# A causal attention stage that computes its own relative products, with the mask added on PE

## The chip, the cores and the metric

The kernel runs on one core of a Trainium2 chip. The metric is the time of one execution on the device in microseconds (us), as the median over several runs. The whole program is a decoder of four gated layers; the change touches only the attention of layer 0.

## The reference, cut to what matters

Layer 0's attention has 16 heads of 16 channels over 8 sequences of 512 rows. Queries come from the stream, keys and values from a context. To every score a relative term is added: the product of the query with a table `Er`, skewed so that the column says how far back the key lies. A causal mask follows, and the softmax.

```python
def _skew(QEr):
    B, H, R, C = QEr.shape
    padded = jnp.pad(QEr, ((0, 0), (0, 0), (0, 0), (1, 0)))
    reshaped = padded.reshape(B, H, C + 1, R)
    return reshaped[:, :, 1:, :]
# q, k, v: (8, 16 heads, 512, 16)
QEr = q @ Er.T
Srel = _skew(QEr)
attn = (q @ k.T + Srel) / 4      # then -inf where the key lies after the query
out = softmax(attn, axis=-1) @ v
```

## The kernel before, in words

The program is a row of phases, each with its own buffers and semaphores; a barrier of all engines ends each. Three phases bear on the change. There are 8 batches (sequences) of 16 heads, 128 heads in all, and a head has four query tiles t = 0..3 of 128 rows; by causality tile t has (t + 1) * 128 key columns, so its tiles are 128, 256, 384 and 512 wide.

**`qkv` (names `a_`).** For each batch it normalises the rows, makes Q and K transposed in four jobs (two of K, two of Q, 128 channels each), and splits each float32 result on DVE into three bf16 parts (L255 to L259, one after the other). `parts` has two buffers, so the split of job j waits until the store of job j - 2 has landed. SP stores a job with one DMA at L190. The dram tensors `k_parts` and `q_parts` hold the three parts one after the other.

**`rel_scores` (names `r_`).** A product of 96 rows stands for a float32 product of 16 channels: six pairs of bf16 parts (`TERMS`), 16 rows each, are stacked on the partitions. POOL loads Q for a batch with six DMAs, each onto 16 partitions (L1273). PE multiplies each of the four tiles of a head with the table (L1307), DVE and ACT copy two tiles each out of PSUM (L1333, L1354), and SP writes the head to the dram tensor `rel` (L1286), 128 x 1280 float32, 640 KB, through a ring of four buffers.

**`causal_attention` (names `t_`).** POOL loads Q and K, each with six DMAs onto 16 partitions (L3797), one pair every second head, and V (L3793). SP reads a head of `rel` back with the skew done by the address pattern (L3756), into one of four tiles `relsb`. POOL adds the mask `M` to the diagonal blocks of that tile (L3822). The rest is a software pipeline written out by hand in steps; step u stands for one tile of one head, u = 4 * head + t, and every engine walks through the steps in order:

- PE: the score product of unit u + 4 (L3850), the transposes of unit u (L3857), and at t = 1 four of the 16 value products of the group of four heads before (L3869).
- DVE: for unit u + 3 the sum of scores and relative part, with its row minimum (L3896); at t = 0 and 2 the copy of the transposed tile u out of PSUM (L3745); once per group the copy of the output (L3902).
- ACT: exp of unit u + 3 (L3923); at t = 1 and 3 the copy of the transposed tile (L3745).

The transposed tiles have two PSUM buffers, one for even and one for odd t. PE's transposes of unit u wait for the exp of u and for the copy of u - 2:

```python
wait(pe, "expo", u.n + 1)
wait(pe, "cp_act" if u.t % 2 else "cp_dve", u.head * 2 + u.t // 2)
```

Of the kernel before, what the change touches and what calls it, by code (L numbers as in the profile page):

```python
# [32 lines left out]
def alone(eng):  # L33

    eng.nop(nofuse=True)
# [97 lines left out]
def qkv(nc, G, name, src, jobs, weights, vjob, ctx=None, affine=None, tile_k=None, nlog=0):  # L133
# [11 lines left out]
    nj = len(jobs)  # L145
    scaled = sorted({(j[3], j[4]) for j in jobs if j[3] and j[4] != 1.0})
    with phase(nc, name, "w c0 c1 c_free stats rstd xn xn_free xt_ps xt_ps_free xt xt_free "
# [21 lines left out]
        with nc.Block() as block:  # L169

            @block.sync
            def _(sp):
# [33 lines left out]
                sp.wait_ge(s["parts_st0"], 16 + 16 * NB * ((nj + 1) // 2))  # L206
                sp.wait_ge(s["parts_st1"], 16 + 16 * NB * (nj // 2))
# [18 lines left out]
            def _(dve):  # L226
# [20 lines left out]
                def split(b, before):  # L247
                    ch.at(before)
                    for j in range(nj):
# [4 lines left out]
                        dve.wait_ge(s[f"parts_st{j % 2}"], b * (16 * k) + 16 * (j // 2) + 16)  # L254
# [122 lines left out]
def attention(nc, G, name, qs, ks, vs, H, DH, blocks, masks, odst, sums, rel=None):  # L377

    NC = max(1, 6 * DH // P + (6 * DH % P > 0)) if DH < 64 else 3
    TPC = 6 // NC
    KR = TPC * DH
    HD, VW = H * DH, DH + 1
    GH = 4
    NG = H // GH  # L400
    SCORES, EXPO, TURN = 7, 6, 4
    width = [(blocks(t)[1] - blocks(t)[0]) * P for t in range(NT)]
    OFF = [sum(width[:t]) for t in range(NT)]
    WMAX = max(width)

    users = [[t for t in range(NT) if blocks(t)[0] <= kb < blocks(t)[1]] for kb in range(NT)]
    windowed = WMAX < S
    UW = WMAX if windowed else S
    nload = 13
    with phase(nc, name, "in0 in1 loaded qk_free vh vones rel0 rel1 score least expo turned cp_dve cp_act pv "  # L410
               "o_free o_st0 o_st1") as (s, sb, ps):
        Q = sb("Q", [P, 2, NC, H, S], BF16)
        K = sb("K", [P, 2, NC, H, S], BF16)
        V = sb("V", [P, 2, NT, HD])
        Vh = sb("Vh", [P, GH, NT, VW])
        prob = sb("prob", [P, NT, WMAX])
        expT = sb("expT", [P, 2, NT * UW])
        nmax = sb("nmax", [P, 2, NT])
        osb = sb("osb", [VW, GH, S])
        if rel is not None:  # L420
            relsb = sb("relsb", [P, 2, sum(width)])
            summed = sb("summed", [P, NT, WMAX])
        sps = ps("sps", [P, NT, S])
        tps = ps("tps", [P, 2, S])
        ops = ps("ops", [VW, 2, S])

        class Unit:


            def __init__(self, p, it, h, j, t, n, pair, first):  # L430

                self.p, self.it, self.h, self.slot, self.t, self.n, self.pair, self.first = p, it, h, j % GH, t, n, pair, first

        def walk(eng, step, head):

            def early(m):
                def at(k):
                    h, t = divmod(m + k, NT)
                    return Unit(0, 0, h, h, t, h, h // 2, False) if m + k >= 0 else None
                return at  # L440

            def group(p, it, g, final):
                b = it * 2 + p
                for i in range(GH):
# [11 lines left out]
            for m in range(-SCORES, 0):  # L456
                step(early(m))
# [3746 lines left out]
```

## Time and profile before

| | |
|---|---|
| Median of 3 runs | 6249.43 us (6245.49 to 6275.58) |
| Profiled execution, first to last instruction | 6247.0 us |
| PE, DVE, ACT, POOL busy over the span | 74%, 63%, 46%, 33% |
| `qkv` of layer 0 | about 18 to 167 us |
| `rel_scores` | about 167 to 459 us |
| `causal_attention` | about 459 to 1079 us |
| all later phases | from 1079 us |

The profiled execution is 2.4 us shorter than the median of the runs. Busy shares over the whole span say little here, since the phases follow one another and the change reaches three of them; each has to be read in its own window.

### The profile page before, as it was taken

The page shows a single profiled execution, that of the slowest core. Times are in us where ns is not written, and L with a number is a line of the kernel's source. Part 1 is how long each engine was busy: PE and PEld are TensorE (multiplying, and loading weights), DVE is VectorE, ACT ScalarE, POOL GpSimd, SP SyncE. Part 2 cuts the span into 40 slices and gives each one's busy share as a digit, 9 for nine tenths or more (in the row PEclk, how much of TensorE's full clock was granted, in tenths as well). Part 3 has the DMA queues.
Part 4 walks back from the last instruction along what each step waited for, and adds up shares of the span by engine and source line. Part 5 has one row for each costly group of instructions (what it writes and reads, how often), then busy time and mean ns, then how long its engine had stood idle before and what let it go on. Part 6 is the DMA issues. An engine that isn't in the chain of part 4 may idle for free. (4 is left out here: it accounts for less than half of the span.)

```text
span 6247.0 us, 101680 instructions
## 1 busy us (share of the span) xinstructions
PE 4641.5 (74%) x24902; PEld 2868.6 (46%) x24902; DVE 3907.9 (63%) x8145; ACT 2867.3 (46%) x6151; POOL 2042.9 (33%) x3122
## 2 busy tenths in 40 slices
PE   7455666493879973998676767797677887995897
PEld 4113333342643331885234645686555663333433
DVE  6344555538547875443678956558866556886565
ACT  2235655215227753223564556435456323773353
POOL 0113443000036630221443554124542214542342
PEclk9558989696988986999778989998889998997897
DMA  4999986100063321111551232002321115332533
GB/s 158 283 360 190 211 197 157 45 0 0 0 201 89 97 63 45 43 43 41 155 144 62 102 115 65 27 13 92 129 73 41 28 49 182 92 85 82 179 117 100
DMA packets 317791, 648.30 MB, mean 104 GB/s; under 512 B 73170, under 2 KB 128115, under 8 KB 317384
## 3 DMA queue, kind: packets, MB, share of 16 engines
q1 hardware_dynamic: 245912, 450.68, 22.7%
q0 software_dynamic: 71488, 193.32, 13.1%
q8 instruction: 134, 2.20, 0.1%
q14 instruction: 257, 2.11, 0.1%
HBM read 373.99 MB, written 238.70 MB: 98 GB/s over the span
## 5 line engine op out<-in xcount | busy, mean ns | idle before, releaser
L1115 DVE TENSOR_REDUCE t_nmax<-t_aps 128x2 f32<-128x1024 f32 x700 | 838.0, 1221 | 278.2 <-PE t_aps L1037 272.6
L1222 ACT ACTIVATE t_expT<-t_bps 128x512 f32<-128x512 f32 x1290 | 700.9, 599 | 284.4 <-PE t_bps L1056 235.4
L1056 PE MATMUL t_bps<-t_Q,t_K 51*128 51x512 f32 (+2 forms) x1290 | 525.9, 468 | 60.8 <-ACT t_expT L1222 43.8
L1037 PE MATMUL t_aps<-t_K,t_Q 49*128 49x512 f32 (+2 forms) x1400 | 464.7, 460 | 64.7 <-DMA t_K<-k_halves 28.9
L1056 PEld LDWEIGHTS t_bps<-t_Q,t_K 51*128 51x128 f32 (+2 forms) x1290 | 228.8, 189 | 528.6 <-ACT t_expT L1222 373.5
L2517 DVE TENSOR_TENSOR f_hl<-f_h,f_hh 128x512 fp32r<-128x512 f32 x192 | 203.7, 1061 | 413.3 <-ACT f_hh L2442 413.3
L1083 PE MATMUL t_ops<-t_expT,t_V 128*17 128x512 f32 (+1 forms) x2560 | 414.2, 614 | 0.5 <-ACT t_expT L1222 0.4
L3923 ACT ACTIVATE t_relsb<-t_relsb,t_nmax 128x128 f32<-128x128 f32 (+3 forms) x515 | 277.6, 559 | 272.8 <-DVE t_nmax L3896 264.0
L3857 PE MATMUL t_tps<-ident,t_relsb 128*128 128x128 f32 x1280 | 246.6, 296 | 160.1 <-ACT t_expT L3745 149.3
L2806 POOL TENSOR_TENSOR a_crossed<-a_qsb,a_tab 128x256 f32<-128x256 f32 x272 | 268.1, 1007 | 295.9 <-ACT a_qsb L2753 271.3
L1156 POOL DMA_DIRECT2D t_Q<-q_halves x525 | 270.9, 518 | 143.9 <-POOLq L78 72.9
L3822 POOL TENSOR_TENSOR t_relsb<-t_relsb,t_M 128x128 f32<-128x128 f32 (+1 forms) x384 | 198.5, 546 | 335.5 <-DMA t_relsb<-rel 304.0
L3896 DVE CUSTOM_DVE_ANT_0 t_relsb<-t_sps,t_relsb 128x128 f32<-128x128 f32 (+3 forms) x515 | 234.0, 484 | 83.6 <-PE t_sps L3850 52.6
L3573 ACT ACTIVATE t_prob<-t_summed,t_nmax 128x256 f32<-128x256 f32 (+1 forms) x560 | 265.6, 479 | 26.9 <-DVE t_nmax L3625 22.3
L3857 PEld LDWEIGHTS t_tps<-ident,t_relsb 128*128 128x128 f32 x1280 | 169.0, 150 | 231.4 <-issue 215.7
L1156 POOL DMA_DIRECT2D t_K<-k_halves x525 | 267.5, 512 | 18.6 <-issue 10.3
L3515 PE MATMUL t_tps<-ident,t_prob 128*128 128x128 f32 x964 | 151.7, 303 | 154.4 <-DVE t_prob L3640 154.3
L3583 ACT COPY t_expT<-t_tps 128x512 f32<-128x512 f32 (+1 forms) x276 | 144.3, 523 | 262.6 <-PE t_tps L3515 262.6
L1037 PEld LDWEIGHTS t_aps<-t_K,t_Q 49*128 49x128 f32 (+2 forms) x1400 | 214.5, 199 | 103.8 <-issue 52.4
L1307 PE MATMUL r_o<-r_erk,r_Q 96*128 96x128 bf16 (+3 forms) x512 | 161.0, 460 | 133.2 <-DVEq L1335 92.8
L3745 DVE COPY t_expT<-t_tps 128x128 f32<-128x128 f32 (+1 forms) x256 | 108.0, 422 | 197.9 <-PE t_tps L3857 197.7
L2382 PE MATMUL f_yps<-f_wdh,f_hh 128*128 128x256 f32 x768 | 217.9, 284 | 13.8 <-DVE f_hl L2517 13.8
(441 smaller groups left out, 12543.1 us busy)
## 6 DMA issues: line engine op xcount, KB each, us to landing
rel<-r_out SPq DMA_DIRECT2D x128, 640.0 KB, 5.4
t_relsb<-rel SPq DMA_DIRECT2D x128, 640.0 KB, 5.6
t_Q<-q_halves POOLq DMA_DIRECT2D x420, 64.0 KB, 2.5
t_K<-k_halves POOLq DMA_DIRECT2D x420, 64.0 KB, 2.5
k_halves<-a_parts SPq DMA_DIRECT2D x48, 512.0 KB
q_halves<-a_parts SPq DMA_DIRECT2D x48, 512.0 KB, 5.6
o_xT<-attended SPq DMA_DIRECT2D x32, 512.0 KB, 4.3
f_R<-combine SPq DMA_DIRECT2D x128, 128.0 KB, 3.0
```

What stands on the lines that cost most here:

```text
L1037: last = nc.tensor.matmul(aps[:, (t * PPG + i) % 2, x, :], operand(Qr, KA, p, h, slice(t * P, (t + 1) * P)), operand(Kr, KA, p, h, slice(0 ...
L1056: nc.tensor.matmul(bps[:, slot_of(kb, j), :], operand(Kr, KB, p, h, slice(kb * P, (kb + 1) * P)), operand(Qr, KB, p, h, slice(0, S)), star ...
L1083: last = nc.tensor.matmul(ops[j * COL:j * COL + VW, :], V[:, p, kb, g * HG + j, :], expT[:, kb % RING, j, :], start=kb == 0, stop=kb == NT ...
L1115: nc.vector.tensor_reduce(nmax[:, g, t, i * HPT:(i + 1) * HPT], aps[:, (t * PPG + i) % 2], AX.X, ALU.max, negate=True).then_inc(s["maxed"], 1)
L1156: pool.dma_start(dst[o + i * DH:o + (i + 1) * DH, p, cols], rows(src, part, r, g, b)).then_inc(sem, 16)
L1222: nc.scalar.activation(expT[:, kb % RING, j, :], bps[:, slot_of(kb, j), :], ACT.Exp).then_inc(s["expo"], 1 + (PAD if end else 0))
L2382: last = nc.tensor.matmul(o, fast(x), fast(w), start=m == 0 and i == 0 and t % 2 == 0, stop=m == NF - 1 and i == 2, skip_group_check=True)
L2806: last = nc.gpsimd.tensor_tensor(y[:, :, k, :], x[:, :, 1 - k, :], tab[:, 2 * i + 1, t, k * HW:(k + 1) * HW].unsqueeze(1).broadcast_to([P, ...
L3573: nc.scalar.activation(prob[:, u.slot, i, x, 0:w], summed[:, u.slot, i, x, 0:w], ACT.Exp, scale=-1.0, bias=nmax[:, u.slot, i, x:x + 1], ac ...
L3857: last = nc.tensor.transpose(tps[:, u.t % 2, kb * P:(kb + 1) * P], u.tile()[:, kb * P:(kb + 1) * P], G.ident[:, :])
L3896: nc.vector.tensor_tensor_reduce(out=u.tile(), in0=sps[:, u.t, 0:u.w], in1=u.tile(), scale=1.0, scalar=3.0e38, op0=ALU.add, op1=ALU.min, a ...
L3923: nc.scalar.activation(u.tile(), u.tile(), ACT.Exp, scale=-1.0, bias=nmax[:, u.j, u.t:u.t + 1]).then_inc(s["expo"], 1)
```

## The change: what it does

`rel_scores` and `causal_attention` become one phase, `relative_attention`. On the same steps u, PE now also computes a relative product, that of unit u + 24 (six heads ahead, `AHEAD = 6`), after the transposes; its four tiles are taken in the order 3, 1, 0, 2 and go to two PSUM buffers. `keep_rows` copies them out at the end of a step: on DVE the tiles of 512 and 128 columns, on ACT those of 256 and 384. SP writes a head (`spill`, three buffers `rows`), and two heads later reads it back skewed (`skew`, five tiles `relsb`). The scores have three PSUM buffers in place of four, the output one in place of two.

POOL no longer adds the mask. For each score tile PE computes the diagonal block apart and accumulates onto it the product of an identity with the mask.

`qkv` stores a job with six DMAs, which write the six stacked terms of every head to `k_terms` or `q_terms`, [16 heads, 96, 4096]. Q and K are then loaded with four DMAs each of 96 partitions and four heads, and Q once and not twice. The loops are written out; the empty instruction behind each wait (`alone`) is gone. The old general `attention` function, which nothing called, is deleted.

```diff
 # qkv, SP: the store of one job
-                        sp.dma_start(dst.rearrange("r f t -> f r t")[row:row + P, :, ds(b * S, S)],
-                                     parts[:, j % 2]).then_inc(s[f"parts_st{j % 2}"], 16)
+                        h = row // 16
+                        for i, term in enumerate(TERMS):
+                            part = term[dst is not qdst] - 1
+                            sp.dma_start(dst[h:h + P // 16, i * 16:(i + 1) * 16, ds(b * S, S)], parts[:, j % 2, part]).then_inc(s[f"parts_st{j % 2}"], 16)
...
-def rel_scores(nc, G, name, qs, er, rel):
...
-def causal_attention(nc, G, name, qs, ks, vs, rel, odst, sums):
+def relative_attention(nc, G, name, qs, ks, vs, er, rel, odst, sums):
...
+    AHEAD = 6
+    SB, RS, RING = 3, 3, 5
+    ORDER = (3, 1, 0, 2)
...
+        def keep_rows(eng, op, n, i, what):
+
+            t = ORDER[i]
+            wait(eng, f"st{n % RS}", 16 * (n // RS))
+            eng.wait_ge(s["product"], n * NT + i + 1)
+            op(rows[:, n % RS, OFF[t]:OFF[t] + WIDTH[t]], rps[:, i % 2, 0:WIDTH[t]]).then_inc(s[what], 1)
...
+                def spill(n):
+                    if n >= NH:
+                        return
+                    sp.wait_ge(s["kept_d"], n * 2 + 2)
+                    sp.wait_ge(s["kept_a"], n * 2 + 2)
+                    sp.dma_start(rel[n:n + 1, :].rearrange("o (p c) -> (o p) c", c=RW), rows[:, n % RS, :]).then_inc(s[f"st{n % RS}"], 16)
+
+                def skew(n):
+                    if not 0 <= n < NH:
+                        return
+                    sp.wait_ge(s[f"st{n % RS}"], 16 * (n // RS + 1))
+                    wait(sp, "turned", (n - RING + 1) * NT)
+                    x = rel[n:n + 1, P - 1:]
+                    sp.dma_start(relsb[:, n % RING, :], bass.AP(x.tensor, x.offset, [[RW - 1, P], [1, RW]])).then_inc(s[f"rel{n % RING}"], 16)
...
+                for n in range(NH + 2):
+                    spill(n)
+                    skew(n - 2)
...
-                    qp, kp = TERMS[r]
-                    for dst, part, src in ((Q, qp, qs), (K, kp, ks)):
-                        pool.dma_start(dst[r * DH:(r + 1) * DH, p], src[part - 1].rearrange("(h d) t -> d h t", d=DH)[:, :, ds(b * S, S)]).then_inc(s[f"in{p}"], 16)
+                    if r < 2 * QH:
+                        dst, src, what = ((Q, qs, "q"), (K, ks, "k"))[r // QH]
+                        h = r % QH * (H // QH)
+                        pool.dma_start(dst[:, p, h:h + H // QH, :], src.rearrange("h r t -> r h t")[:, h:h + H // QH, b * S:(b + 1) * S]).then_inc(s[f"{what}{p}"], 16)
...
-                    wait(pe, "least", u.n - NT + 1)
-                    nc.tensor.matmul(sps[:, u.t, 0:u.w], Q[0:KR, u.p, u.h, u.t * P:(u.t + 1) * P], K[0:KR, u.p, u.h, 0:u.w],
-                                     start=True, stop=True).then_inc(s["score"], 1)
+                    wait(pe, "least", u - SB + 1)
+                    q, diag = Q[:, b % 2, h, t * P:(t + 1) * P], sps[:, u % SB, t * P:(t + 1) * P]
+                    if t:
+                        nc.tensor.matmul(sps[:, u % SB, 0:t * P], q, K[:, b % 2, h, 0:t * P], start=True, stop=True)
+                    nc.tensor.matmul(diag, q, K[:, b % 2, h, t * P:(t + 1) * P], start=True, stop=False)
+                    nc.tensor.matmul(diag, G.identb[:, :], G.masks[:, 2, :], start=False, stop=True).then_inc(s["score"], 1)
...
+                def relative(u):
+                    n, i = unit(u)
+                    if n is None:
+                        return
+                    b, h = divmod(n, H)
+                    t = ORDER[i]
+                    if h == 0 and i == 0:
+                        pe.wait_ge(s[f"q{b % 2}"], 16 * QH * (b // 2 + 1))
+                    wait(pe, "kept_a" if i % 2 else "kept_d", n * 2 + i // 2)
+                    nc.tensor.matmul(rps[:, i % 2, 0:WIDTH[t]], Q[:, b % 2, h, t * P:(t + 1) * P], erk[:, S - WIDTH[t]:S],
+                                     start=True, stop=True).then_inc(s["product"], 1)
...
+                def step(u):
+                    scores(u + SCORES)
+                    turn(u)
+                    relative(u + AHEAD * NT)
+                    n, t = unit(u)
+                    if n is not None and t == 1 and n >= HG:
+                        values(n // HG - 1, n % HG)
...
             @block.scalar
+                def step(u):
+                    n, t = unit(u + EXPO)
+                    if n is not None:
+                        act.wait_ge(s["least"], u + EXPO + 1)
+                        nc.scalar.activation(tile(n, t), tile(n, t), ACT.Exp, scale=-1.0, bias=nmax[:, n % RING, t:t + 1]).then_inc(s["expo"], 1)
+                    n, t = unit(u)
+                    if n is not None and t % 2:
+                        copied(act, nc.scalar.copy, n, t, "cp_act")
+                    m, i = unit(u + AHEAD * NT - 1)
+                    if m is not None and i % 2:
+                        keep_rows(act, nc.scalar.copy, m, i, "kept_a")
```

On PE, in the middle of the attention, one head before reads so (`t_sps` are the scores, `t_tps` the transposed tiles, `t_ops` the output; the register instructions of the loop stand between):

```order
L3850 MATMUL t_sps<-t_K,t_Q 128x256
L3857 MATMUL t_tps<-ident,t_relsb 128x128 x2
L3869 MATMUL t_ops<-t_expT,t_Vg 17x384 x4
L3733 REGISTER_ALU
L3850 MATMUL t_sps<-t_K,t_Q 128x384
L3733 REGISTER_ALU
L3857 MATMUL t_tps<-ident,t_relsb 128x128 x3
```

The same steps t = 1 and t = 2 on PE after the change (`t_rps` are the relative products):

```order
L3407 MATMUL t_sps<-t_K,t_Q 128x128
L3408 MATMUL t_sps<-t_K,t_Q 128x128
L3409 MATMUL t_sps<-masks,identb 128x128
L3418 MATMUL t_tps<-ident,t_relsb 128x128 x2
L3430 MATMUL t_rps<-t_erk,t_Q 128x256
L3442 MATMUL t_ops<-t_expT,t_Vg 17x128 x4
L3407 MATMUL t_sps<-t_K,t_Q 128x256
L3408 MATMUL t_sps<-t_K,t_Q 128x128
L3409 MATMUL t_sps<-masks,identb 128x128
L3418 MATMUL t_tps<-ident,t_relsb 128x128 x3
L3430 MATMUL t_rps<-t_erk,t_Q 128x128
```

Between the two transposes of step 1 and the three of step 2 there is now a relative product, and the one score product has become three.

On ACT one head in the same place before the change, exps and copies of transposed tiles:

```order
L3923 ACTIVATE t_relsb<-t_relsb,t_nmax 128x384
L3745 COPY t_expT<-t_tps 128x4x128
L3923 ACTIVATE t_relsb<-t_relsb,t_nmax 128x512
L3923 ACTIVATE t_relsb<-t_relsb,t_nmax 128x128
L3745 COPY t_expT<-t_tps 128x2x128
L3923 ACTIVATE t_relsb<-t_relsb,t_nmax 128x256
```

And after it, with the relative rows copied to `t_rows`:

```order
L3510 ACTIVATE t_relsb<-t_relsb,t_nmax 128x384
L3312 COPY t_expT<-t_tps 128x4x128
L3510 ACTIVATE t_relsb<-t_relsb,t_nmax 128x512
L3319 COPY t_rows<-t_rps 128x384
L3510 ACTIVATE t_relsb<-t_relsb,t_nmax 128x128
L3312 COPY t_expT<-t_tps 128x2x128
L3510 ACTIVATE t_relsb<-t_relsb,t_nmax 128x256
L3319 COPY t_rows<-t_rps 128x256
```

Two copies have come in, one between the exps of 512 and 128 columns, one after that of 256.

## Rows read from the trace of the kernel before

**Rows 1.** The page's head; busy time (instructions) of each engine by window, clock, DMA, GB/s.

```profile
span 6247.0 us, 101680 instructions
...
core 0: us, PE busy (x) PEld busy (x) DVE busy (x) ACT busy (x) POOL busy (x), PEclk, DMA share, GB/s
18.00:167.00 149.00, 125.58 (x384) 66.34 (x384) 109.96 (x256) 40.04 (x65) 10.15 (x16) 0.93 0.44 146
167.00:459.00 292.00, 160.98 (x512) 53.67 (x512) 116.32 (x261) 96.44 (x256) 30.54 (x55) 0.50 0.97 331
459.00:501.00 42.00, 0.50 (x3) 0.39 (x4) 1.21 (x3) 0.00 (x0) 10.02 (x18) 0.50 0.97 150
501.00:1079.00 578.00, 399.00 (x2818) 219.81 (x2816) 332.89 (x1318) 349.67 (x771) 257.13 (x504) 0.93 0.83 194
```

**Rows 2.** The same view: short stretches with one kind of transfer under way.

```profile
87.00:88.00 1.00, 1.00 (x5) 0.66 (x4) 0.97 (x2) 0.02 (x1) 0.00 (x0) 1.00 0.71 254
...
182.00:190.00 8.00, 0.00 (x0) 0.00 (x0) 0.00 (x0) 0.00 (x0) 0.84 (x2) 0.50 1.07 112
...
210.00:222.00 12.00, 10.02 (x32) 3.33 (x32) 6.92 (x16) 5.98 (x16) 0.00 (x0) 0.50 1.02 422
...
1020.00:1050.00 30.00, 20.41 (x154) 11.35 (x154) 18.04 (x75) 18.95 (x43) 12.16 (x25) 1.00 0.51 164
```

**Rows 3.** Timeline, one head period: start, duration, engine, line, out<-in, [idle before <-releaser].

```profile
1063.45 0.41 PE L3857 MATMUL t_tps<-ident,t_relsb 128*128 128x128 f32 x2 [1.16 <-ACT t_expT L3745]
1063.79 0.84 PE L3869 MATMUL t_ops<-t_expT,t_Vg 128*17 128x384 f32 x8
...
1064.56 0.34 PE L3850 MATMUL t_sps<-t_K,t_Q 96*128 96x384 bf16 x1
...
1064.73 0.49 PE L3857 MATMUL t_tps<-ident,t_relsb 128*128 128x128 f32 x3
...
1065.33 0.56 DVE L3745 COPY t_expT<-t_tps 128x384 f32<-128x384 f32 x1 [1.84 <-PE t_tps L3857]
...
1065.80 0.55 DVE L3896 CUSTOM_DVE_ANT_0 t_relsb<-t_sps,t_relsb 128x384 f32<-128x384 f32 x1
...
1066.45 0.61 ACT L3923 ACTIVATE t_relsb<-t_relsb,t_nmax 128x384 f32<-128x384 f32 x1 [1.57 <-DVE t_nmax L3896]
...
1066.98 0.56 ACT L3745 COPY t_expT<-t_tps 128x512 f32<-128x512 f32 x1
...
1067.44 1.01 ACT L3923 ACTIVATE t_relsb<-t_relsb,t_nmax 128x512 f32<-128x512 f32 x2
...
1067.68 0.41 PE L3857 MATMUL t_tps<-ident,t_relsb 128*128 128x128 f32 x2 [1.16 <-ACT t_expT L3745]
```

**Rows 4.** Groups by shape in `rel_scores` and in the attention (count | busy, mean ns | idle).

```profile
L1333 DVE COPY r_out<-r_o 128x512 f32<-128x512 f32 x122 | 83.0, 680 | 0.0
...
L1354 ACT COPY r_out<-r_o 128x384 f32<-128x384 f32 x122 | 59.2, 485 | 0.0
...
L3850 PE MATMUL t_sps<-t_K,t_Q 96*128 96x128 bf16 x126 | 29.3, 232 | 55.1 <-POOLq L3812 49.2 <-issue 5.9
```

**Rows 5.** Who waited for whom, 480 to 1060 us: total, times, longest.

```profile
DVE t_expT L3745 <- PE t_tps L3857: 190.9, 114, 3.3
PE t_tps L3857 <- ACT t_expT L3745: 145.8, 135, 2.1
...
DVE t_relsb L3896 <- POOL t_relsb L3822: 28.7, 20, 3.5
```

**Rows 6.** DMA issues and us to landing, 168 to 466 us.

```profile
rel<-r_out SPq DMA_DIRECT2D x128, 640.0 KB, 5.4
...
r_Q<-q_parts POOLq DMA_DIRECT2D x48, 256.0 KB, 10.7
```

**Rows 7.** The writes of `rel` alone, time to landing.

```profile
DMA to landing us min/median/max: 5.0/5.4/14.2
```

**Rows 8.** `qkv`: two jobs on DVE in the timeline, then the stores' landings.

```profile
83.29 0.42 DVE L255 CAST a_parts<-a_q 128x512 bf16<-128x512 f32 x1
...
86.40 0.43 DVE L255 CAST a_parts<-a_q 128x512 bf16<-128x512 f32 x1 [0.33 <-DVE a_parts L259]
...
89.58 0.43 DVE L255 CAST a_parts<-a_q 128x512 bf16<-128x512 f32 x1 [0.37 <-DMA k_parts<-a_parts]
...
DMA to landing us min/median/max: 3.2/3.2/3.9
```

**Rows 9.** SP issues DMAs back to back; the end of the attention (timeline).

```profile
18.58 0.46 SPq L177 DMA_DIRECT2D a_wk<-in_L_xattn_Wk  x1
19.08 0.46 SPq L177 DMA_DIRECT2D a_wv<-in_L_xattn_Wv  x1
...
1078.43 0.69 DVE L3902 COPY t_osb<-t_ops 128x512 f32<-128x512 f32 x1 [3.62 <-PE t_ops L3869]
```

**Rows 10.** The start of `rel_scores` (timeline).

```profile
171.73 0.41 DVE L1321 CAST r_pbf<-r_r 16x512 bf16<-16x512 f32 x1
172.45 2.89 POOL L1267 DMA_DIRECT2D r_erk<-r_pbf  x6 [4.64 <-DVE r_pbf L1321]
175.49 4.11 POOL L1273 DMA_DIRECT2D r_Q<-q_parts  x7 [0.15 <-issue]
...
193.02 2.33 PE L1307 MATMUL r_o<-r_erk,r_Q 96*128 96x128 bf16 x8 [35.91 <-DMA r_Q<-q_parts]
```

More of the change, by code:

```diff
@@ L129, in _, with qkv @@
                 sp.wait_ge(s["stored"], 16)
[L133 removed]
+def qkv(nc, G, name, src, jobs, weights, vjob, qdst, ctx=None, affine=None, tile_k=None, nlog=0):
     nj = len(jobs)
+    ST = 16 * len(TERMS)
     scaled = sorted({(j[3], j[4]) for j in jobs if j[3] and j[4] != 1.0})
@@ L3715, in walk @@
[L3715 to L3728 removed]
+        rps = ps("rps", [P, 2, S])
@@ new lines, in walk, with unit, copied @@
+        def walk(step):
+            for u in range(-(AHEAD + 1) * NT, NH * NT):
+                step(u)
+        def unit(u):
+            return divmod(u, NT) if 0 <= u < NH * NT else (None, None)
+        def copied(eng, op, n, t, what):
+            g = n // HG
+            if n % HG == 0 and t < 2:
+                wait(eng, "pv", g - 1)
+            eng.wait_ge(s["turned"], n * NT + t + 1)
+            x = expT[:, g % 2, n % HG, t * P:t * P + 1]
+            dst = bass.AP(x.tensor, x.offset, [list(x.ap[0]), [PITCH, t + 1], [1, P]])
+            op(dst, tps[:, t % 2, 0:WIDTH[t]].rearrange("p (k q) -> p k q", q=P)).then_inc(s[what], 1)
@@ L3883, in _, with link @@
+                pe.wait_ge(s["erp"], 96)
+                walk(step)
                 for kb in range(NT):
-                    values(NB * NG - 1, 1, kb)
+                    values(NGT - 1, kb)
             @block.vector
             def _(dve):
-                nc.vector.tensor_copy(M[:, :], G.masks[:, 2, :]).then_inc(s["mask"], 1)
-                nc.vector.memset(ops[:, :, :], 0.0).then_inc(s["zero"], 1)
+                def link(ins, n):
+                    ins.then_inc(s["chain"], 1)
+                    dve.wait_ge(s["chain"], n)
@@ L3915, in _ @@
-                keep(NB * NG - 1, 1, NB // 2 - 1, NB * NG // 2 - 1)
+                    n, t = unit(u)
+                    if n is None:
+                        return
+                    if t == 0:
+                        dve.wait_ge(s[f"rel{n % RING}"], 16 * (n // RING + 1))
+                    dve.wait_ge(s["score"], u + 1)
+                    nc.vector.tensor_tensor_reduce(out=tile(n, t), in0=sps[:, u % SB, 0:WIDTH[t]], in1=tile(n, t), scale=1.0, scalar=3.0e38,
+                                                   op0=ALU.add, op1=ALU.min, accum_out=nmax[:, n % RING, t:t + 1]).then_inc(s["least"], 1)
@@ L3917, in _ @@
+                walk(step)
+                keep(NGT - 1)
             @block.scalar
             def _(act):
-                def step(at):
-                    u = at(EXPO)
-                    if u:
-                        wait(act, "least", u.n + 1)
-                        nc.scalar.activation(u.tile(), u.tile(), ACT.Exp, scale=-1.0, bias=nmax[:, u.j, u.t:u.t + 1]).then_inc(s["expo"], 1)
-                    u = at(0)
-                    if u and u.t % 2:
-                        copied(act, nc.scalar.copy, u, "cp_act")
@@ L3931, in normalise_turn @@
+                walk(step)
 def normalise_turn(nc, G, name, src, dst):
```

617 lines of the change are left out of this document (105 added, 512 removed).

## The prediction

> **What bounds the kernel now.** I read the windows by phase first [rows 1]. Between 167 and 459 us the DMA engines are busy 0.97 of the time and PE only 161 of 292 us: `rel_scores` is bound by its transfers. From 459 to 501 us no engine computes, and again the DMA share is 0.97: the loads of the first batch. From 501 to 1079 us no engine is full: PE 399, ACT 350, DVE 333 of 578 us, DMA 0.83. Such a phase is bound by a loop of waits between engines, so I read the waits next: DVE waits 191 us for transposed tiles, PE waits 146 us for ACT's copies of them, and only 29 us go to the late relative tile [rows 5].
>
> The timeline shows the loop [rows 3]. PE's two transposes (t = 1) start at 1063.45, the value products at 1063.79, the score at 1064.56, the three transposes at 1064.73, DVE's copy of them at 1065.33, the next sum at 1065.80, its exp at 1066.45, ACT's copy of the 512 tile at 1066.98, and that frees the buffer for the transposes of the next head at 1067.68. The period is 0.34 + 0.77 + 0.17 + 0.60 + 0.47 + 0.65 + 0.53 + 0.70 = 4.23 us. The real mean from 501 to 1079 us is 578 / 128 = 4.5 us a head [rows 1]: some heads wait for a tile from POOL (28.7 / 128 = 0.22 us each [rows 5]), and the clock is at 0.93, not 1.00.
>
> Of the transfers I read three rates [rows 2]. Writes of `rel` run at 422 GB/s. Skewed reads alone give 164 GB/s at a share of 0.51, so 320 GB/s while they run. Loads of Q onto 16 partitions run at only 112 GB/s and keep the engines at 1.07: 3.1 MB of Q and K for a batch take 28 us of all the DMA engines. The Trainium skill ("SBUF — State Buffer", The DMA port swizzle) says that partitions 0 to 15 reach 4 of 16 ports and measured 104 GB/s; this trace agrees with its 112 GB/s. By that page 96 partitions reach all ports and the new loads should run nearly three times as fast.
>
> **What goes.** The three windows from 167 to 1079 us, 912 us [rows 1].
>
> **What it costs now: the new loop.** Relative product i of a head waits for the copy of product i - 2. The one that matters is i = 1 (256 columns), which stands on PE between the transposes of step 1 and the value products. It waits for ACT's copy of the 384-wide product (i = 3), and ACT does this one after the exp of the 512 tile, after the copy of the 512 tile. So the old link "ACT copy starts to transposes start, 0.70, and 0.34 more to the values" becomes: copy to exp 0.46 [rows 3], exp of 512 columns 0.62 (the pair takes 1.01 [rows 3]; I give the 128 one 0.39), copy of 384 columns 0.485 [rows 4] and 0.13 for the signal (0.70 less the copy's 0.56, rounded): 1.70 us in place of 1.04, +0.66.
>
> The relative product itself occupies PE for about 0.12 us (a 384-wide score frees PE after 0.17 [rows 3]). The score of this step has the same 384 columns plus a mask product. No row shows a mask product: below it costs 128 columns, 0.06 us, above an isolated product of that width, 0.232 us [rows 4]; it stands back to back with others, so I take 0.12 with the split. Every fourth head DVE's copy of the output (0.69 [rows 9]) stands before the sum of the 512 tile and delays its exp by about 0.4: 0.1 a head. The loop is 4.23 + 0.66 + 0.12 + 0.12 + 0.10 = 5.2 us. The other relative products fall in PE's idle time ahead of the freed buffer, 1.16 us a head [rows 3].
>
> Engine work stays under this: DVE has 332.9 / 128 = 2.6 us a head plus 0.68 and 0.29 for its rows, 3.6; ACT 2.7 plus 0.86, 3.6; PE 3.1 plus four products and four masks, at most 8 x 0.232, 5.0 if nothing overlaps, about 4 if it does. The mask leaves POOL (257 us of work) and gains nothing by itself, as POOL waited for its loads most of the time; only the 0.22 us of late tiles may shrink. I let these and the slower stretches of the clock stand at +0.1: **5.3 us a head**.
>
> DMA per head: write 655 KB at 422 GB/s 1.55 us; skewed read at 320 GB/s 2.05; Q and K 197 KB, between 112 GB/s (1.75) and the 358 GB/s of 1 KB stores (254 at a share of 0.71 [rows 2]; 0.55), and I take 0.8; V and output 0.1. That is 4.5 us, below 5.3, with ends of 4.25 and 5.45.
>
> **Start and end.** Today the first product comes 26 us after the phase begins, held by the loads of Q [rows 10]. Now Q is issued at once and the table's chain ends near 178 us. Head 0 is written after 3 us, lands 5.4 us later [rows 6], and is read back in some 6: the first sum about 24 us into the phase. Then 122 heads at 5.3 and the last six, which have no relative products left, at 4.3: 672 us. The last value products and copy take about 5 [rows 9]. New phase: 24 + 672 + 5 = 701 us against 912: **-211**.
>
> **`qkv`.** DVE takes 3.1 us for a job (83.29 to 86.40) and a store lands in 3.2, so with two buffers it waits 0.37 us [rows 8]. Now six DMAs carry 786 KB. The fixed part of the landing is 3.2 less 393 KB at 358 GB/s, 2.1 us. Below, the transfer is as long as six issues on SP, five spacings of 0.50 us [rows 9] and the last piece at 358 GB/s, 2.9: job 2 of a batch waits about 1.5 us more, +12 us over 8 batches. Above, it runs at the 112 GB/s of the slow loads, 7.0 us a job: 28 for the jobs and 2.9 for the other megabyte make 31 us a batch against today's 17.5 to 18, +105. Neither shape is like the new one (8 x 16 x 512), and I take the middle, 4.7 us: job 2 starts 6.8 after job 0's end, job 3 4.7 after that, and a batch takes 22.5 us, +5, so **+40**.
>
> The Trainium skill ("DMA: Bandwidth & Descriptors", Why a DMA increments its semaphore by 16 and not by 1) has a rule against this change: a DMA runs on the largest number of engines up to 16 that divides the slowest dimension of both sides. Here these are 8 and 128, so 8 engines would serve each store. At half of 358 GB/s that is 4.4 us a job and about +37 us; by the plain rate of the rows the term would be +12 and the whole 28 us better. No row before shows such a shape.
>
> Sum: 6247 - 211 + 40 = 6076 us for the profiled execution, about 6078 as a median of runs (2 us more, as today).
>
> **The rivals.**
> - *The wait for ACT's copy doesn't bind* (the removed empty instructions shorten each handover, or signals overlap). Then the loop is the old one plus 0.24: 4.5 us a head, 122 x 0.8 = 98 us less: 5980. For it: three handovers in the loop, each with 0.1 or more. Against: the order of instructions is strict. 0.15.
> - *The transfers bind.* If 1 KB pieces and not the 16 partitions are what is slow, Q and K cost 1.75 us a head and all DMA 5.45; with bursts (writes wait up to 14.2 us today [rows 7]) 5.9 us a head: +73, 6150. For it: the DMA share of 0.83 to 0.97 in all windows from 167 us. Against: 1 KB stores ran at 358 GB/s [rows 2]. 0.20.
> - *Slower than before: the round trip through `rows`.* A head's four copies are spread over three steps, 0.75 of a head period, and the slot is needed again after 3 periods, so a write must land within 2.25 periods. The gain is gone when the period reaches 5.3 + 169 / 122 = 6.7, that is when writes land in 15 us on average, and at 15.7 us it is slower by over 0.5%. The median is 5.4, the maximum 14.2 [rows 7], under the slow loads. SP also queues each skewed read behind the next write's wait, so a late copy delays both. 0.06; about 6300.
> - *Little is moved* (the two phases' costs add up again, 6.5 us a head): 6220 to 6280. 0.04.
>
> **Numbers.** The likeliest case (0.55) is 6078, with its own range of 6040 (stores at the lower bound) to 6140 (stores between middle and upper). With half of the first rival and nearly all of the second the range is 5975 to 6170. Below 0.5% (31 us) a measurement of this kernel tells little from no change. Faster by more than that: 0.55 + 0.15 + 0.20, and a little of the rest, 0.91; within it 0.03; slower 0.06.
>
> **What would show it.** In the new profile: ACT's copy of the 384 product is what PE's relative product of 256 columns waits for, about 0.5 us or more a head; DVE's longest wait stays the one for transposed tiles; heads come every 5.3 us; the loads of Q and K land in well under 10.7 us [rows 6] and DMA is near 0.85, not 1.0. In `qkv` DVE waits for the stores by some 5 us a batch. The prediction is wrong if the period is set by the skewed read or by the write of `rows` (DVE or ACT waiting on a DMA), if PE's work and not a wait fills the loop, or if `qkv` grows by 12 or by 100 us.

## The result, and the profile after

| | before | after |
|---|---|---|
| Median of runs | 6255.79 us (4 runs) | 6079.80 us (6057.82 to 6096.23, 4 runs) |
| Profiled execution | 6247.0 us | 6056.2 us |
| Ratio, with its 95% interval | | 0.9717 (0.9688 to 0.9747) |

The change makes the kernel 2.8% faster; 6078 was predicted. The profiled execution after is the fastest of its four.

The windows of the changed kernel come first, in the columns of [rows 1]: `qkv`, the start of `relative_attention` up to its first sum, and from the first to the last sum. The last row is a stretch of `qkv` in which only the new stores run.

```profile
18.00:220.00 202.00, 137.58 (x384) 71.94 (x384) 109.93 (x256) 40.14 (x65) 10.15 (x16) 0.81 0.54 170
220.00:249.00 29.00, 9.07 (x30) 2.77 (x30) 8.34 (x19) 4.25 (x10) 10.80 (x17) 0.50 0.91 256
249.00:892.00 643.00, 494.02 (x4146) 291.31 (x4145) 422.65 (x1551) 424.34 (x1010) 54.55 (x94) 0.96 0.88 303
...
90.00:99.00 9.00, 8.93 (x30) 4.73 (x28) 5.57 (x15) 1.37 (x2) 0.41 (x2) 1.00 0.51 155
```

`qkv` now ends at 220 us and not at 167: 53 us lost. The attention ends with DVE's last copy of the output at 898.8 us (1079.1 before [rows 9]), so all that lies between the end of `qkv` and there takes 679 us and not 912: 233 won. Together that is 180 us. The profiled execution is 191 us shorter; the other 11 us lie in later phases whose code is the same, and are scatter between two executions (the runs of either kernel lie up to 38 us apart).

One head period of the changed kernel, from the timeline of all engines, to be held against [rows 3]:

```profile
640.88 0.56 ACT L3312 COPY t_expT<-t_tps 128x512 f32<-128x512 f32 x1
...
641.34 0.72 ACT L3510 ACTIVATE t_relsb<-t_relsb,t_nmax 128x512 f32<-128x512 f32 x1
...
641.59 0.41 PE L3418 MATMUL t_tps<-ident,t_relsb 128*128 128x128 f32 x2 [0.45 <-ACT t_expT L3312]
641.97 0.47 ACT L3319 COPY t_rows<-t_rps 128x384 f32<-128x384 f32 x1
...
642.49 0.28 PE L3430 MATMUL t_rps<-t_erk,t_Q 96*128 96x256 bf16 x1 [0.49 <-ACT t_rows L3319]
...
642.70 0.84 PE L3442 MATMUL t_ops<-t_expT,t_Vg 128*17 128x384 f32 x8
...
643.47 0.28 PE L3407 MATMUL t_sps<-t_K,t_Q 96*128 96x256 bf16 x1
...
643.71 0.50 PE L3418 MATMUL t_tps<-ident,t_relsb 128*128 128x128 f32 x3
...
644.25 0.56 DVE L3312 COPY t_expT<-t_tps 128x384 f32<-128x384 f32 x1 [1.76 <-PE t_tps L3418]
...
644.72 0.55 DVE L3482 CUSTOM_DVE_ANT_0 t_relsb<-t_sps,t_relsb 128x384 f32<-128x384 f32 x1
...
645.31 0.62 ACT L3510 ACTIVATE t_relsb<-t_relsb,t_nmax 128x384 f32<-128x384 f32 x1 [1.65 <-DVE t_nmax L3482]
...
645.83 0.57 ACT L3312 COPY t_expT<-t_tps 128x512 f32<-128x512 f32 x1
```

From one copy of the 512 tile (640.88) to the next (645.83) are 4.95 us. The reader is to see the row at 642.49: the transposes ahead of it were done, but PE stands 0.49 us until ACT has copied the 384 columns of the relative product, and the value products, the next scores and the next transposes are queued behind.

The waits from 260 to 880 us (in total, times, longest) say the same for all heads:

```profile
DVE t_expT L3312 <- PE t_tps L3418: 189.4, 116, 3.3
...
PE t_rps L3430 <- ACT t_rows L3319: 71.7, 124, 0.9
...
PE t_tps L3418 <- ACT t_expT L3312: 54.4, 122, 0.9
...
DVE t_relsb L3482 <- DMA t_relsb<-rel: 23.3, 20, 2.5
...
PE t_rps L3430 <- DVE t_rows L3319: 17.4, 102, 0.8
```

PE's wait for the freed buffer was 146 us before [rows 5]; now 54 are left, and 72 stand at the relative product behind it. DVE still waits longest for transposed tiles. The DMA issues and landings from 200 to 900 us:

```profile
rel<-t_rows SPq DMA_DIRECT2D x128, 640.0 KB, 4.5
t_relsb<-rel SPq DMA_DIRECT2D x128, 640.0 KB, 6.5
t_Q<-q_terms POOLq DMA_DIRECT2D x32, 384.0 KB, 5.7
```

The loads of Q carry 384 KB in 5.7 us where 256 KB took 10.7 [rows 6].

### The profile page after: what moved, and what is told of

Same layout as the page of the kernel before. It is cut to its first block and busy times, and to the rows that moved or that the text cites. A ratio compares the mean times of both kernels' runs of the same rounds, so it can differ in the third digit from the quotient of the medians.

```text
span 6056.2 us, 95752 instructions
## 1 busy us (share of the span) xinstructions
PE 4601.5 (76%) x25794; PEld 2900.3 (48%) x25794; DVE 3893.5 (64%) x8138; ACT 2853.8 (47%) x6148; POOL 1810.4 (30%) x2657
## 5 line engine op out<-in xcount | busy, mean ns | idle before, releaser
L3430 PE MATMUL t_rps<-t_erk,t_Q 96*128 96x512 bf16 (+3 forms) x512 | 160.3, 316 | 136.6 <-ACT t_rows L3319 72.5
L3205 DVE CUSTOM_DVE_ANT_0 t_summed<-t_sps,t_M 128x256 f32<-128x256 f32 (+1 forms) x568 | 188.0, 384 | 58.6 <-PE t_sps L3084 57.1
L1962 PE MATMUL f_yps<-f_wdh,f_hl 128*128 128x256 f32 x768 | 217.4, 283 | 0.0
```

Of the source, the lines that this page charges most:

```text
L1962: last = nc.tensor.matmul(o, fast(x), fast(w), start=m == 0 and i == 0 and t % 2 == 0, stop=m == NF - 1 and i == 2, skip_group_check=True)
```

## The experiments

All ran beside the kernel before. The ratio is to it; "sums" is the time from DVE's first to its last sum of scores and relative part, 643 us in the changed kernel (248.7 to 891.8). It leaves the scatter of the other phases out, so small effects are read there. It comes from one profiled execution of each kernel; how much it scatters can be seen from two pairs that differ only in the layout of Q and K: row_major and the changed kernel lie 0.6 us apart, vf_rm and values_first 0.9.

| run | median us | ratio (95%) | `qkv` ends | sums |
|---|---|---|---|---|
| the changed kernel | 6079.8 | 0.9717 (0.9688 to 0.9747) | 220.7 | 643.1 |
| values_first | 6021.9 | 0.9619 (0.9594 to 0.9644) | 219.6 | 583.7 |
| small_act | 6066.9 | 0.9686 (0.9662 to 0.9710) | 222.0 | 633.2 |
| no_mask | 6071.7 | 0.9696 (0.9671 to 0.9721) | 222.4 | 644.1 |
| pool_mask | 6067.2 | 0.9694 (0.9666 to 0.9721) | 221.4 | 639.3 |
| row_major | 6036.5 | 0.9626 (0.9593 to 0.9659) | 178.4 | 643.7 |
| old_loads | 6056.6 | 0.9670 (0.9641 to 0.9698) | 167.0 | 663.4 |
| nops | 6124.7 | 0.9778 (0.9750 to 0.9806) | 221.4 | 688.8 |
| vf_rm | 5959.6 | 0.9512 (0.9483 to 0.9540) | 178.9 | 582.8 |
| vf_rm_noload | 5931.8 | 0.9470 (0.9440 to 0.9500) | 179.2 | 543.1 |
| vf_rm_ahead7 | 5956.8 | 0.9507 (0.9489 to 0.9524) | 180.1 | 563.2 |

The theory is that of the prediction: a loop of waits sets the period, now led through ACT's copy of the 384 relative columns. The rivals are the transfers, PE's own work, and DVE's.

### values_first: does that wait set the period?

```diff
                     turn(u)
-                    relative(u + AHEAD * NT)
                     n, t = unit(u)
                     if n is not None and t == 1 and n >= HG:
                         values(n // HG - 1, n % HG)
+                    relative(u + AHEAD * NT)
```

> One line of PE's order changes: the relative product of a step now stands behind the value products instead of ahead of them. Theory (the loop through ACT's copy of the 384 columns sets the period): in the changed kernel PE waits 0.49 us a head at the 256-column relative product with the value products queued behind it. Now the value products fill that wait, so the link from ACT's copy of the 512 tile to the score falls from 1.61 + 0.21 to about 0.71 + 0.34 + 0.21: the period falls by 0.4 to 0.55 us a head, the phase from 679 to about 620 us. Rival (the transfers set the period; their share was 0.89 to 0.93): the period stays within 0.15 us of 5.0 and the share is near 1.

The sums take 583.7 us, 59 less, 0.46 a head, within the 0.4 to 0.55 expected; all engines do the same work in another order. The theory holds. But the DMA share in the window of its sums has risen from 0.88 to 0.97:

```profile
247.00:831.00 584.00, 474.00 (x4151) 286.86 (x4148) 422.93 (x1551) 431.38 (x1009) 54.57 (x94) 0.97 0.97 334
```

### small_act: the length of the copy in the loop

```diff
-    ORDER = (3, 1, 0, 2)
+    ORDER = (3, 1, 2, 0)
```

> The order of the relative tiles is 3, 1, 2, 0 in place of 3, 1, 0, 2: DVE copies 512 and 384 columns out, ACT 256 and 128, and the copy that PE's 256-column relative product waits for has 128 columns in place of 384. Theory (loop through this copy): the copy takes 0.29 in place of 0.47 us, so the period falls by about 0.18 us a head, 22 us in all, although DVE gets 0.2 us of work more. Rival (transfers or DVE's work set the period): no change, or slower by up to 25 us.

The sums fall by 10 us, less than half of the 22 expected, in the theory's direction. Its timeline shows where the rest is. ACT's exp of the 512 tile had followed its own copy after 0.46 us; with 384 columns to copy, DVE makes the sum late, and the exp starts 0.56 us after the copy (row 1 to row 3). ACT's copy of 128 columns, the last row, could start at 647.14.

```profile
645.96 0.56 ACT L3312 COPY t_expT<-t_tps 128x512 f32<-128x512 f32 x1
...
646.40 0.08 DVE L3482 DVE_READ_ACCUMULATOR2_ANT t_nmax<- 128x1 f32 x1
...
646.52 0.72 ACT L3510 ACTIVATE t_relsb<-t_relsb,t_nmax 128x512 f32<-128x512 f32 x1
...
647.14 0.24 ACT L3319 COPY t_rows<-t_rps 128x128 f32<-128x128 f32 x1
```

So a second path, through DVE, lies 0.1 us behind the first; a rival by which DVE's added work would make it slower is out. By the medians of whole runs alone the gain is not clear of noise (0.9686 against 0.9717, intervals that overlap); it rests on the sums.

### no_mask and pool_mask: the mask product

no_mask leaves the causal mask out inside the diagonal blocks:

```diff
-                    if t:
-                        nc.tensor.matmul(sps[:, u % SB, 0:t * P], q, K[:, b % 2, h, 0:t * P], start=True, stop=True)
-                    nc.tensor.matmul(diag, q, K[:, b % 2, h, t * P:(t + 1) * P], start=True, stop=False)
-                    nc.tensor.matmul(diag, G.identb[:, :], G.masks[:, 2, :], start=False, stop=True).then_inc(s["score"], 1)
+                    nc.tensor.matmul(sps[:, u % SB, 0:WIDTH[t]], Q[:, b % 2, h, t * P:(t + 1) * P], K[:, b % 2, h, 0:WIDTH[t]],
+                                     start=True, stop=True).then_inc(s["score"], 1)
```

> Leaves the causal mask out: one score product per tile as before the change, no mask product (so the softmax also sees the keys after the query inside the diagonal block, and the output differs). Theory (a loop of waits, PE has room): of the seven extra instructions a head only the two of the 384-column score lie in the loop, 0.24 against 0.17 us from score to transposes, so the period falls by 0.05 to 0.1 us, 6 to 12 us in all. Rival (PE's own work fills the period): seven times 0.06 us, 0.4 us a head and 50 us in all.

The sums take 644.1 us, 1 more, where 6 to 12 less were expected. The mask products cost nothing that can be seen in the sums, so PE's work doesn't fill the period. The windows of the sums of no_mask and of pool_mask show a lower granted clock than the 0.96 of the changed kernel, with PE less busy:

```profile
250.00:894.00 644.00, 490.04 (x3254) 264.59 (x3254) 422.64 (x1553) 422.74 (x1009) 54.79 (x94) 0.90 0.89 303
```

```profile
250.00:890.00 640.00, 480.46 (x3254) 257.42 (x3254) 426.39 (x1553) 429.77 (x1010) 249.52 (x477) 0.93 0.89 304
```

The trace allows a closer look. Of the 117 periods from head 4 to head 121 (from one 128-column sum to the next), 102 passed wholly at the full granted clock in the changed kernel, and only 70 in no_mask. Those 70 took 4.92 us on average, those 102 took 4.98: 0.05 less, at the lower end of what was expected, but no larger than its own uncertainty (a standard error of 0.05). So the small gain may be there and a lower clock in the other heads may have taken it back; why the clock fell is not shown.

pool_mask undoes the second half of the change's title alone, within the merged phase: the scores as in no_mask, and POOL adds `M` to the tile read back.

```diff
+                def mask(n):
+                    if n >= NH:
+                        return
+                    pool.wait_ge(s[f"rel{n % RING}"], 16 * (n // RING + 1))
...
+                                last = nc.gpsimd.tensor_tensor(z, z, m, ALU.add)
+                    last.then_inc(s["masked"], 1)
...
-                        dve.wait_ge(s[f"rel{n % RING}"], 16 * (n // RING + 1))
+                        dve.wait_ge(s["masked"], n + 1)
```

> The changed kernel with the mask added by POOL to the diagonal blocks of the tile read back, as before the change, and one score product per tile; the rest of the merged phase is as changed. Theory (the move of the mask is worth next to nothing): the period stays at 5.0 us, the time from the first to the last sum within 10 us of 643. The three additions of POOL (1.55 us) fall between the landing of a tile and its use, where the changed kernel waits 25.6 us in all, so up to 15 us more are possible. Rival (the mask on PE is what made the merged phase cheap, since the chain landing, POOL, DVE is gone): over 1 us a head, 100 us or more.

639.3 against 643.1 us: within the 10 us expected of the theory. Moving the mask to PE bought nothing by itself inside the merged phase; the gain lies in the rest of the change.

### row_major: the stores of `qkv`

```diff
-        qs = dram("q_terms", [16, 96, TOK], BF16)
+        qs = dram("q_terms", [D, 6, TOK], BF16)
...
-                            sp.dma_start(dst[h:h + P // 16, i * 16:(i + 1) * 16, ds(b * S, S)], parts[:, j % 2, part]).then_inc(s[f"parts_st{j % 2}"], 16)
+                            sp.dma_start(dst[row:row + P, i, ds(b * S, S)], parts[:, j % 2, part]).then_inc(s[f"parts_st{j % 2}"], 16)
...
-                        pool.dma_start(dst[:, p, h:h + H // QH, :], src.rearrange("h r t -> r h t")[:, h:h + H // QH, b * S:(b + 1) * S]).then_inc(s[f"{what}{p}"], 16)
+                        pool.dma_start(dst[:, p, h:h + H // QH, :], src.rearrange("(h d) i t -> (d i) h t", d=DH)[:, h:h + H // QH, b * S:(b + 1) * S]).then_inc(s[f"{what}{p}"], 16)
...
-                    pool.dma_start(erk[i * DH:(i + 1) * DH, :], erp[:, kp - 1, :]).then_inc(s["erp"], 16)
+                    pool.dma_start(erk[i:i + (DH - 1) * 6 + 1:6, :], erp[:, kp - 1, :]).then_inc(s["erp"], 16)
```

> The two dram tensors of terms are laid out as 256 rows x 6 terms, the 96 partitions of Q, K and the table hold row * 6 + term, so that each of the six stores of a job writes 128 rows of one stride (128 x 512) in place of 8 x 16 x 512. Same bytes, same count of stores and loads. Theory (the 8 x 16 x 512 stores run on half of the DMA engines: 160 GB/s at a share of 0.5): the layer's qkv phase ends near 180 us in place of 220, 40 us less, and the attention phase is the same within 6 us. Rival (six issues on SP or the doubled bytes make it slow): qkv still ends above 210 us.

`qkv` ends at 178.4 us, 42 us earlier, with the same bytes in the same number of DMAs, and the sums stay at 643.7. In the changed kernel DVE waited 51.1 us for these stores; here, from 20 to 180 us, it waits 15.4:

```profile
DVE a_parts L257 <- DMA k_terms<-a_parts: 15.4, 16, 1.5
```

With the stores alone under way the changed kernel moved 155 GB/s at a DMA share of 0.51 (the window 90 to 99 us above). That reads as half of the engines busy all the time, not as all of them busy half of the time: in the packet records of that stretch most often 8 packets are in flight and never more than 12, in row_major (91 to 98 us) most often 16. A job's 786 KB at 155 GB/s take 5.1 us. By the rule of the Trainium skill ("DMA: Bandwidth & Descriptors", Why a DMA increments its semaphore by 16 and not by 1) 8 x 16 x 512 against 128 rows is served by 8 engines; the 0.51 agrees.

The edit also changed how long SP takes to issue a store. The first row is the changed kernel's, the second row_major's, each the twelve stores of two jobs:

```profile
80.87 9.91 SPq L194 DMA_DIRECT2D k_terms<-a_parts  x12
```

```profile
90.11 6.15 SPq L193 DMA_DIRECT2D k_terms<-a_parts  x12
```

That is 0.83 us a store against 0.51. Six issues at 0.83 make 5.0 us a job, next to the 5.1 of the transfers. So the shape is shown to be the cause, but no run tells whether the 8 engines alone, with fast issues, would have cost as much.

### old_loads: what the new layout of Q and K buys

The merged phase with the old `k_parts` and `q_parts`, one store per job and loads onto 16 partitions.

```diff
-    ST = 16 * len(TERMS)
+    ST = 16
...
+                        sp.dma_start(dst.rearrange("r f t -> f r t")[row:row + P, :, ds(b * S, S)],
+                                     parts[:, j % 2]).then_inc(s[f"parts_st{j % 2}"], 16)
...
-    QH = 4
+    QH = 6
...
+                        i = r % QH
+                        pool.dma_start(dst[i * DH:(i + 1) * DH, p], src[TERMS[i][r // QH] - 1].rearrange("(h d) t -> d h t", d=DH)[:, :, b * S:(b + 1) * S]).then_inc(s[f"{what}{p}"], 16)
```

> The changed kernel with the layout, the stores and the loads of Q and K of the kernel before: one store of three parts per job, and per batch six loads of Q and six of K, each onto 16 partitions (12 in place of 8, at heads 2 to 13). Theory (transfers onto 16 partitions run at 112 GB/s whatever else goes on, and this is what the new layout buys): qkv ends near 167 us again, 53 less, but all transfers of a head come to about 5.5 us, above the loop's 5.0, so the time from the first to the last sum rises from 643 to 700 or 760 us; in all from no change to 60 us more. Rival (the loads are hidden whatever their shape): from first to last sum 643 us again, and 50 us less in all.

Both were off. `qkv` ends at 167.0 us, as expected. The sums take 663.4 us, 20 more: the slow loads are not hidden, but far from the 57 or more that I expected. The first sum comes 41 us into the phase and not 28. In all the attention ends 21 us earlier than in the changed kernel. So the layout as the change made it lost more in `qkv` (54 us) than it won behind it (33 us). The medians of the whole runs say the same, 23 us, but with intervals that overlap (0.9670 against 0.9717). From 250 to 800 us the writes and reads of `rel` land in 7.1 and 10.0 us (4.5 and 6.6 from 300 to 800 us in the changed kernel), and from 300 to 780 us DVE waits 104 us for the tile read back:

```profile
rel<-t_rows SPq DMA_DIRECT2D x104, 640.0 KB, 7.1
t_relsb<-rel SPq DMA_DIRECT2D x104, 640.0 KB, 10.0
```

```profile
DVE t_relsb L3480 <- DMA t_relsb<-rel: 104.4, 60, 3.9
```

That much of this wait falls into slack which the loop at ACT's copy leaves anyway is argued, not shown. My sum of 5.5 us of transfers a head was too high as well: the period was 663.4 / 127.75 = 5.2 us. The trace shows which term of it was wrong, the 112 GB/s. The queue of POOL's loads reads so while Q was loaded alone in the kernel before (182 to 190 us), and in old_loads from 250 to 800 us (packets, MB, share of the 16 engines):

```profile
q0 software_dynamic: 273, 0.89, 106.6%
```

```profile
q0 software_dynamic: 7123, 23.71, 19.6%
```

Alone, 0.89 MB took 8 us at a share of 1.07: 104 GB/s, once divided by the share. Mixed with the writes and reads of `rel`, 23.71 MB (3.7 of them V) took a share of 0.196 of 550 us: 220 GB/s, so divided. Such a load kept the engines for about half as long per byte when other transfers ran beside it; why is not shown. With 220 in place of 112 my sum would have been 4.6 us a head.

### nops: the empty instructions behind the waits

```diff
                 eng.wait_ge(s[what], n)
+                alone(eng)
...
                     pe.wait_ge(s["expo"], u + 1)
+                    alone(pe)
...
                     dve.wait_ge(s["score"], u + 1)
+                    alone(dve)
```

Such a line stands behind each wait of PE, DVE and ACT in the phase, 18 lines in all; one of them is in a helper that POOL and SP use too. The kernel before had one behind nearly every wait of its causal half, but behind only some of those of its relative products, so the run puts back somewhat more than the change took out.

> The changed kernel with an empty instruction behind every wait of PE, DVE, ACT and POOL in the attention phase, as the kernel before had them. Theory (the handovers of the loop, 0.54 and 0.59 us now against 0.60 and 0.65 before the change, are shorter because these are gone): 0.05 us for each of four or five handovers in the loop, so 0.2 to 0.3 us a head, 643 to about 670 us from the first to the last sum. Rival (they cost nothing where an engine waits anyway): within 5 us of 643.

The sums take 688.8 us: 45.7 more, 0.36 a head, somewhat above the expected 0.2 to 0.3. Against the 176 us of the change that is a quarter, and an upper bound for what dropping them brought. With them the merged phase takes 727 us (221.4 to 948.0), still 185 less than the 912 before. Even if its 48 us and the 33 us of the new layout (old_loads) simply add up, some 150 of the 233 us won behind `qkv` are left, by this estimate, for the merging itself; no run has the two phases apart and the rest of the change. The window shows the lower clock again (0.91 for 0.96):

```profile
249.00:938.00 689.00, 522.23 (x4152) 324.53 (x4150) 424.69 (x1553) 423.48 (x1010) 55.61 (x94) 0.91 0.84 283
```

Counted as for no_mask, 80 of the 117 periods passed wholly at the full clock, and they took 5.12 us on average (median 5.15) against 4.98 (4.95) for the 102 of the changed kernel. So 0.15 to 0.20 us a head, some 20 to 25 us, is the empty instructions themselves; the rest of the 0.36 stands in periods with lower clock.

### vf_rm, vf_rm_noload, vf_rm_ahead7: both gains together, and the next bound

vf_rm has the edits of values_first and row_major.

> Value products ahead of the relative product (as in values_first) and the row * 6 + term layout (as in row_major) together. Theory (the two gains are in different phases): both add up, qkv ends near 178 us and from the first to the last sum it takes about 584 us, so some 5980 us as a median. Rival (faster heads now wait for the transfers, whose share was 0.98 in values_first, and the new layout loads a little differently): the sums take over 600 us.

They add up: 5959.6 us, ratio 0.9512 (0.9483 to 0.9540), 120 us below the changed kernel. `qkv` ends at 178.9 us and the sums take 582.8. This version beats both kernels.

The next run keeps Q and K of the first two batches for all later ones, which so compute with the wrong data; PE's waits for the loads are cut down to match:

```diff
-                    if b + 1 < NB and 2 <= h <= 2 * QH + 2:
+                    if b + 1 < NB and 2 <= h <= 2 * QH + 2 and (b < 1 or h == 2 * QH + 2):
```

> As vf_rm, but Q and K are loaded for the first two batches alone, and the later batches compute with these (their output differs); V is loaded as before. That leaves out 0.2 MB a head. Theory (in values_first, at a DMA share of 0.98 and 4.55 us a head, the transfers have become the bound): the period falls to the loop of the engines, about 4.3 us, 20 to 35 us less from the first to the last sum than in vf_rm. Rival (the loop of waits still sets the period, and the high share only means that transfers queue): the same within 6 us.

The sums fall by 40 us to 543.1, 4.25 us a head: in vf_rm the loads of Q and K do cost time. The last run asks for each head's tile earlier, with no byte less:

```diff
-    AHEAD = 6
+    AHEAD = 7
```

> vf_rm with relative products seven heads ahead in place of six, so every write and read back of a head has one period more. Theory (in vf_rm the bandwidth of the transfers is the bound, share 0.95 to 0.98): within 6 us of the 583 us from the first to the last sum, since no byte less is moved. Rival (latency: the tiles land late only because they are asked for late): DVE's wait for tiles, 72 us between 300 and 780, goes away, and 20 to 40 us with it.

The sums fall by 20 us, to 563.2, more than bandwidth alone would allow, and DVE's wait for the tile read back (72 us in vf_rm) is no longer among its long ones. But a wait of 34 us for the writes of the three `rows` buffers takes its place, from 300 to 780 us:

```profile
DVE t_rows L3318 <- DMA rel<-t_rows: 33.8, 31, 2.6
```

So about half of those 40 us went to tiles that were asked for too late, and a DMA share of 0.97 was not yet the limit: it is the same in both runs, while 345 GB/s were moved in place of 335. In the whole kernel the 20 us don't show clear of noise (0.9507 against 0.9512, intervals that overlap). The windows of the sums of the three, in this order:

```profile
208.00:790.00 582.00, 471.24 (x4144) 285.80 (x4144) 421.97 (x1549) 431.29 (x1009) 54.58 (x94) 0.97 0.97 335
```

```profile
208.00:752.00 544.00, 456.01 (x4145) 284.63 (x4145) 422.19 (x1553) 423.06 (x1010) 22.71 (x46) 0.99 0.93 323
```

```profile
209.00:772.00 563.00, 463.97 (x4149) 284.88 (x4147) 422.94 (x1551) 424.51 (x1007) 54.78 (x94) 0.99 0.97 345
```

## Why the prediction was right, step by step

**The whole.** 6078 was predicted and 6079.8 measured. The closeness is luck in part: the terms were off by -22 and +13 us, the two profiled executions differ by 11 us more in phases that the change doesn't touch, and the profiled execution after (6056.2) lies 24 us below the median of the runs.

**The new loop (right, confirmed by values_first).** The step said that PE's relative product of 256 columns waits for ACT's copy of 384 and holds the value products behind it. The wait is there with 0.49 us, and running the value products ahead of it gave 59 us. From copy to product I had 1.70 us, and it is 1.61; the product itself holds PE for 0.21 and not 0.12; from score to transposes it takes 0.24 and not 0.29; two handovers take 0.06 less each than before (transposes to copy 0.54, sum to exp 0.59). For the head shown this makes 4.95 us where the terms give 5.13. The mean is 643.1 / 127.75 = 5.03 us; with the last six heads at 4.3 as in the prediction, the others had 5.06 and not 5.3: 29 us too much in the sum.

**The step mis-sized in it** is the empty instructions. I gave their removal only to a rival ("the removed empty instructions shorten each handover"), at 0.15, and nothing to the sum; nops shows 0.15 to 0.20 us a head for them at the full clock and 0.36 with the clock that fell beside them. That is the size of the 0.18 between 5.13 and 4.95. The rival's place was right, its claim that the wait would then not bind was wrong.

**The mask (right, by pool_mask and no_mask).** "Gains nothing by itself": 4 and 1 us. Of the 0.12 us that I charged for the mask product and the split in the loop, 0.07 are in the timeline (0.24 from score to transposes, for 0.17 before).

**The transfers (right as to the bound, too high as a rival).** The DMA share is 0.88 at 5.03 us a head, 4.4 us of transfers where I had 4.5. With a faster loop they come near to binding: a share of 0.97 in values_first, and 40 us less without the loads in vf_rm_noload. The rival "1 KB pieces are slow" fell: the new loads are fast. old_loads, which brings the loads onto 16 partitions back, costs 20 us in the sums where the rival priced them at 73. The price was wrong at its root: I took 112 GB/s from a stretch in which the loads ran alone, and beside other transfers their queue moved 220 GB/s, once divided by its share of the engines.

**Start and end.** 28.0 us to the first sum (24 predicted, though the terms given, 11 + 3 + 5.4 + 6, make 25), since the table's loads landed at 233 us, 12.5 after the phase began, and the first write of relative rows, issued at 235.9, could be read back only from 243.8 on. From first sum to the last copy of the output it took 650 us; 677 predicted.

**`qkv` (right in sign, 13 us too low).** +53 us where I took the middle, +40, between 12 and 105. The stores take 5.1 us a job and not 4.7, and SP spends longer on issuing them than the five spacings of 0.50 us of the lower end: twelve in 9.9 us, 0.83 each. row_major shows that the shape is the cause: with stores of 128 rows, which have both more packets in flight and shorter issues, `qkv` ends 11 us after the old one, next to my lower end of 12.

**The slow rival** (writes of `rows` landing after 15 us) was not near: they land in 4.5 us, 7.9 at most.

**The signs.** PE's relative products wait 124 times for ACT's copies from 260 to 880 us, 72 us in all, 0.58 each (0.5 or more a head forecast). DVE's longest wait is still the one for transposed tiles, heads come every 5.03 us, and PE is busy 494 of 643 us, so its work doesn't fill the loop. In `qkv` DVE waits 51 us for the stores, 6.4 a batch (5 forecast).

**Left open.** Why the granted clock was lower in nops, no_mask and pool_mask; whether the 8 engines or the issues on SP held the stores of `qkv` in the changed kernel, since the two lie within 0.1 us a job; and whether bandwidth or latency holds the half of vf_rm_noload's gain that vf_rm_ahead7 doesn't explain.

## What to carry to other kernels

When work of another phase is put into a loop of waits, find each place where an in-order engine will wait for it, and see what is queued behind: here one line moved past the value products was worth as much as a third of the whole change. Look at what a store's access pattern makes of the DMA engines: the same bytes as 128 rows of one stride took 42 us less than as 8 x 16. And price each part alone: the mask product in the title bought nothing, the dropped empty instructions 20 to 46 us. A rate that was read while one kind of transfer ran alone need not hold beside others.

## What was not expected of the hardware

- An empty instruction behind each wait came with 46 us in 689: 0.36 us a head, with the granted clock at 0.91 for 0.96; in the heads wholly at the full clock it was 0.15 to 0.20 us.
- Leaving out PE work did not speed the phase up: with 892 matrix instructions fewer (3254 for 4146) the granted clock in the window of the sums was 0.90 for 0.96, and the sums took 644.1 us for 643.1.
- A DMA store of 8 x 16 x 512 runs at 155 GB/s with a share of 0.51, those of 128 x 512 in row_major reach up to 355 GB/s in slices of the same stretch, 90 to 99 us.
- Loads onto 16 partitions moved 104 GB/s, divided by their share of the engines, when they ran alone, and their queue 220 GB/s, so divided, beside the traffic of `rel` (old_loads).
